# A two-layer decoder on one core: the engines' loop over turns of four tiles written out as one straight program

## The reference, cut to what matters

```python
x = _layernorm(x + _L0_attn_ref(x, ...))             # 16 heads, latent 32, rotary, causal softmax
x = _layernorm(x + _L0_xattn_ref(ctx_1024, x, ...))  # linear attention: q (k^T v), then its own norm
x = _layernorm(x + _L0_ffn_ref(x, ...))              # weights and activations rounded to FP4 blocks, SiLU gate
x = _layernorm(x + _L1_attn_ref(x, ...))             # causal softmax, and a second, moving-average branch
x = _layernorm(x + _L1_xattn_ref(x, ctx_1024, mask, ...))  # masked cross attention, MLP 1024 wide, two norms
x = _layernorm(x + _L1_ffn_ref(x, ...))              # one 256x256 product rounded to FP6 blocks
```

## Time and profile before

| | |
|---|---|
| time, median of 3 runs | 1191.1 us (1190.35 to 1193.04) |
| profiled execution: span | 1188.5 us |
| profiled execution: its own time | not given apart from the span; the median lies 2.6 us above the span |
| ACT, POOL busy | 43%, 26% of the span |
| instructions with a record | 24,029 |
| DMA | mean 21 GB/s |

### The profile page before, as it was taken

The page is one execution under the profiler, slowest core; times in us unless marked ns, Lnnn a source line. Parts: engine busy times, 40 slices in busy tenths (PEclk is TensorE's granted clock), DMA queues, the critical chain, the costliest instruction groups (busy, mean ns, idle before and its releaser), DMA issues.

```text
span 1188.5 us, 24029 instructions
## 1 busy us (share of the span) xinstructions
PE 977.9 (82%) x8390; PEld 759.2 (64%) x8390; DVE 889.0 (75%) x2135; ACT 509.5 (43%) x1377; POOL 309.3 (26%) x507
## 2 busy tenths in 40 slices
PE   6667778898988898988988898988988898978754
PEld 5445656776666676766676776766666666756633
DVE  3775667888788887868788788868787888877452
ACT  2323436363526354453526354453636354443320
POOL 2561111312222232212222232212222232222021
PEclk9677999999999999989999999989999999999886
DMA  9001000000000000000000000000000000000000
GB/s 344 20 10 68 8 13 9 3 20 8 19 8 15 10 17 10 16 9 8 19 7 15 11 16 10 17 13 4 19 7 15 8 6 6 8 6 5 6 5 4
DMA packets 23854, 24.48 MB, mean 21 GB/s; under 512 B 1728, under 2 KB 22064, under 8 KB 23600
## 3 DMA queue, kind: packets, MB, share of 16 engines
q1 hardware_dynamic: 23728, 22.85, 5.9%
HBM read 18.67 MB, written 2.10 MB: 17 GB/s over the span
## 4 chain that ended last, share of the span: by engine, by line
DVE 35%; PE 35%; issue 13%; ACT 10%; POOL 5%; DMA 0%; DVEq 0%; POOLq 0%; SPq 0%
PE bank L1126 26%; PE bank L1239 9%; ACT prob L664 5%; DVE peak L919 4%; DVE y_ L862 2%; DVE ma_ L1038 2%; ACT prob L658 2%; DVE stats L848 2%; DVE q_top L810 2%; DVE k_ L1062 1%; POOL rstd L523 1%; DVE k_ L1071 1%; POOL k_ L531 1%; DVE x_ L874 1%; DVE scratch L822 1%
## 5 line engine op out<-in xcount | busy, mean ns | idle before, releaser
L664 ACT ACTIVATE prob<-bank,low 128x128 f32<-128x128 f32 x384 | 105.2, 385 | 163.9 <-DVE low L926 163.9
L520 POOL TENSOR_TENSOR var_eps<-mean_var,rsq 128x1 f32<-128x1 f32 x144 | 28.5, 198 | 474.8 <-DVE mean_var L851 474.8
L919 DVE TENSOR_REDUCE peak<-bank 128x4 f32<-128x512 f32 x192 | 126.2, 682 | 31.0 <-PE bank L1126 31.0
L1239 PE MATMUL bank<-cst,prob 128*128 128x128 f32 x768 | 108.7, 287 | 49.4 <-DVE y_ L862 30.3
L1239 PEld LDWEIGHTS bank<-cst,prob 128*128 128x128 f32 x768 | 88.0, 146 | 67.2 <-issue 42.9
L602 ACT ACTIVATE xt_<-bank 128x256 f32<-128x256 f32 x144 | 55.2, 396 | 130.9 <-PE bank L1239 130.3
L602 ACT ACTIVATE probT<-bank 128x512 f32<-128x512 f32 x192 | 102.2, 604 | 10.6 <-PE bank L1239 10.6
L523 POOL TENSOR_TENSOR rstd<-var_eps,rsq 128x1 f32<-128x1 f32 x144 | 79.8, 554 | 11.3
L1126 PE MATMUL bank<-w_gu,xt_ 128*128 128x352 f32 x256 | 80.5, 468 | 1.5 <-ACT w_f L602 1.0
L1126 PE MATMUL bank<-xt_,w 128*128 128x128 f32 x512 | 68.6, 299 | 0.5 <-ACT xt_ L602 0.5
L1126 PEld LDWEIGHTS bank<-xt_,w 128*128 128x128 f32 x512 | 68.2, 218 | 0.9 <-ACT xt_ L602 0.9
(11 more groups left out here) (179 smaller groups left out, 2230.1 us busy)
## 6 DMA issues: line engine op xcount, KB each, us to landing
xtin<-in_xT SPq DMA_DIRECT2D x16, 128.0 KB, 2.2
next_<-in_x SPq DMA_DIRECT2D x16, 128.0 KB, 6.7
ct_<-in_ctxT SPq DMA_DIRECT2D x16, 128.0 KB, 7.5
w<-in_w SPq DMA_DIRECT2D x2, 1024.0 KB, 6.2
out<-x_ SPq DMA_DIRECT2D x16, 128.0 KB, 1.7
next_<-x_ SPq DMA_DIRECT2D x16, 127.0 KB
rowt<-in_rows SPq DMA_DIRECT2D x1, 1664.0 KB, 9.1
w<-in_gate_up SPq DMA_DIRECT2D x2, 512.0 KB, 10.4
```

The lines of the kernel that those rows point to most:

```text
L664: ins = act.activation(prob[:, r, c * P:(c + 1) * P], bank[r][:, c * P:(c + 1) * P], ACT.Exp, scale=SCALES[layer], bias=low[:, b, h:h + 1])
L919: dve.tensor_reduce(peak[:, b, 4 * r:4 * r + 4], rows4(src[:, :]), AX_X, ALU.max)\
L1239: ins = pe.transpose(dst[:, k * P:(k + 1) * P], src[:, k * P:(k + 1) * P], ident)
```

## The change

`run` no longer has a loop. It goes once through `TIMELINE`, which holds all sixteen tiles, and calls each stage with the number of the turn and of the tile within it. Since the turn is now always a number, each wait is on a constant and each address is fixed. Stages, their order, buffers, banks and semaphores stay as they are. The parameters of the engine and of the last turn are dropped from the calls.

```diff
-        def run(eng, table, last=ITERS):
-
-
-            for stage, turn, b in steps_in(0):
+        def run(table):
+
+            for _, stage, t in TIMELINE:
                 if stage in table:
-                    table[stage](turn, b)
-            with eng.Fori(1, last) as i:
-                for stage, turn, b in steps_in(1):
-                    if stage in table:
-                        table[stage]((i, turn - 1), b)
-            for stage, turn, b in [step for n in range(last, ITERS + 1) for step in steps_in(n)]:
-                if stage in table:
-                    table[stage](turn, b)
+                    table[stage](t // GROUP, t % GROUP)
...
-            run(sp, table, last=ITERS - 1)
+            run(table)
...
-            run(pool, table)
+            run(table)
...
-            run(act, table)
+            run(table)
...
-            run(dve, table)
+            run(table)
...
-            run(pe, table)
+            run(table)
```

## The result

| | before | after |
|---|---|---|
| time, median of 11 runs each | 1191.1 us (1188.53 to 1197.83) | 1184.83 us (1180.43 to 1187.86) |
| profiled execution: span | 1188.5 us | 1182.7 us (its own time 1184.83) |
| mean granted clock | 0.938 | 0.936 |
| instructions with a record | 24,029 | 22,289 |

The ratio after to before is 0.994, with a 95% interval of 0.9921 to 0.9959. The change makes the kernel faster, by 6.3 us, which is small (0.6%) but clear of the noise. The forecast was 13.5 us (1177.6), and the result lies 1.8 us above its range of 1173.5 to 1183.0. The sign was right, and so was the mechanism of the jumps; more than half of the gain is missing.

What follows compares the result with a forecast made beforehand. It took the kernel as a chain of short hand-overs, no engine full, stalled by loop jumps. Jumps and pattern 13.2 us plus registers 0.3 gave 13.5 us, from 1191.1 to 1177.6 us, range 1173.5 to 1183.0.

Steps and rivals of the forecast that it cites:

- The jumps: Loop end: two jumps back go, 6.4 us each with stalls and slow clock behind, 12.7 us together.
- The registers: Register arithmetic before waits, mostly covered: at most 0.2 us a tile over twelve tiles, 0 to 2.4 us, 0.3 counted.
- What is late next: Slow-clock stretches in turns 2 and 3 after the edit: turn 1's pattern goes on, gain 12.9 to 13.9 us.
- the drain: Code after the last mark, 131.2 us, already straight: change counted as 0, bound two slow stretches, 2.8 us each way.
- D: Turn ends: no change, the stall comes from loading code there and straight code has it too; 1191 us, chance 3%.
- rival E: Turns 1 to 3: longer straight program's code arrives too late, stalls make it slower, about 1335 us; chance 2%.
- The pattern: Tiles of turns 2 and 3: between two of three and three of four long, 518.7 to 519.6 us for eight.
- B: Turns 2 and 3: all tiles come out long at 65.3 us, gain 10.2, time 1180.9 us; chance 14%.
- A: Turn ends: only PE's stall of 6.1 us comes back, the rest is lost in waits; 1185.0 us, chance 7%.
- C: Tiles and drain: more short tiles or a quicker drain, gain 15 to 20, 1171 to 1176 us; chance 12%.

Runs made afterwards that it cites:

- filled kernels: Unread products put in two idle PE gaps (`x1_turn_h`, `l0_mix`) of the straight and loop kernels: 1160.18 us straight, 1173.9 us loop.
- with the pause moved: Straight kernel with 32 or 64 semaphore increments at the start of DVE's program: 1179.96 us and 1180.58 us.
- its repetition: The changed (straight) kernel run again unmodified, beside the kernels with increments: 1183.75 us, ratio 0.9931 to the kernel before.
- one-jump kernel: Against the kernel before, turn 1 also written out, loop covering only turns 2 and 3, one jump back left: 1188.87 us, ratio 0.9985.
- its filled forms: Loop kernel before with unread products in PE's idle gaps: one filling (`x1_turn_h`) 1184.62 us, two fillings (also `l0_mix`) 1173.9 us.
- DVE-only: Against the kernel before, only DVE's program written out straight, other engines keep the loop: 1195.22 us, ratio 1.0004.
- PE-only: Against the kernel before, only PE's program written out straight, other engines keep the loop: 1186.67 us, ratio 0.9926.
- one-iteration loops: Against the kernel before, turns 1, 2 and 3 as three successive loops of one iteration, folded to constants, no branch taken: 1182.85 us, ratio 0.9927.
- The filled kernel: Straight kernel with two fillings, three unread products in `x1_turn_h` and two in `l0_mix`: 1160.18 us, ratio 0.9702 to the kernel before.

## Why the prediction was wrong

**The jumps, 12.7 us: right within 0.8.** Their stalls are gone, and with the slow stretches filled two of them are worth 11.9. What the prediction hadn't seen is how the price is made: PE's stall sets most of it, and DVE's counts in full only once PE's is gone.

**The registers, 0.3 counted of 0 to 2.4: in its bounds, and counted too low for the filled kernels.** A long tile takes 65.13 us without them and 65.39 or 65.32 with them, and in the filled kernels the remainder of 13.9 - 11.9 = 2.0 us over twelve tiles is theirs by subtraction, net of the straight kernel's two pauses. No run changed them alone. That they run beside the operation in progress holds for DVE in the kernel before: 823 of its 852 register instructions lie inside one of its operations.

**The step that failed: "What is late next".** It took turn 1 and its pattern of slow stretches as given for code that is straight, so turn 1 stood in the sum at no change, and it counted the drain as 0. Three terms went against it, 7.7 us together, the whole of the 13.5 - 5.8 that are missing in the spans:

- 2.1 us in one tile of turn 1: the pause of DVE and the slow stretch behind it. This term was not in the sum at all. The passage at 262.9 us was read as proof that new code costs nothing (against D), and rival E priced each of some 17 packets a turn at 3.07 us. What the trace has lies between the two, 0.37 us at a few places, and one such place sufficed.
- 1.9 us in the other tiles, 0.9 of them in turn 1; the other 1.0 is what turns 2 and 3, with a gain of 12.5, lack to the 13.5. One of twelve tiles came out short (63.73), not three or four. This goes with the pause as well: with the pause moved, the twelve tiles take 778.4 and 778.8 us, which is the forecast's 779.0, and with it in place they take 782.95 and 782.67. So the pause is worth 3.9 to 4.5 us over the twelve tiles, about twice what its own tile shows, and it explains all that they lack. How it works on in the later tiles was not traced.
- 3.6 us in the drain, which was counted as 0 with 2.8 as bound. It took three times 3.4 us of slow clock more, not two, in the changed kernel and again in its repetition. Why the drain fell into this pattern stays open.
- The last 0.1 us lies before the first mark.

**The pattern.** Undisturbed it has the time that was forecast, and that is in part luck, since it is not the pattern that was forecast: two tiles of twelve are short, not three or four, and the long ones take 65.1 us, not 65.3. The register time, counted as a gain, works against itself here. A long tile of 65.13 us comes 0.28 us later against the slow stretches, 64.85 apart, where one of 65.35 came 0.5 later, so it takes longer to slip past them. An estimate from these rows: a short tile of 63.73 gives back 1.12, so four long ones go with one short, and twelve tiles take 12 x (4 x 65.13 + 63.73) / 5 = 778.2 us.

**Rivals.** B (all tiles long) is near in its count, eleven of twelve tiles, but not in its time: it gave turns 2 and 3 a gain of 10.2 us, and they have 12.5, since the long tiles are 0.2 us shorter than B took them. A's number, 1185.0, is met by the median within 0.2 us, and its reason is false: no jump's loss stayed behind. C and D are excluded. E is excluded as a sign; that its cause, code that arrives late, is behind the 0.37 us above is inferred from the places of the pauses, and no run shows it.

**A check of size.** Without the pause the edit gives 11.4 and 10.8 us by the medians (1191.4 - 1179.96 and - 1180.58), without most of the slow stretches 13.7. With both in place it gives 6.3, and 7.7 beside the kernels without the pause. No run tells apart what makes up the rest to 13.7.

## What to carry to other kernels

A stall taken out of a kernel in which an engine's clock drops once in each period of the work need not be worth its length: look where the slow stretches fall now, how far each period slips against them, and count as a possible cost any place like PE's wait here, which a pause of 0.37 us lengthened from 0.50 to 0.87 us and behind which a slow stretch then stood in the changed kernel, though none at 0.86 us in the one-jump kernel. To learn what such an edit is worth by itself, compare both versions with the gaps ahead of the slow stretches filled by products that nobody reads. That filling was here worth about four times the edit: 1191.1 us before, 1184.8 straight, 1160.2 straight and filled (in a group in which before took 1193.6).

## What the runs showed of the hardware that was not expected

- A jump back stalled PE by 3.0 to 3.6 us (before, its filled forms, the DVE-only and one-jump kernels) and DVE by 2.6 to 3.1 (before, its filled forms, the PE-only and one-jump kernels), each in its own program. The branch that fell through took 83 ns on PE before; with three such branches the one-iteration loops took 1182.85 us, beside 1184.83 for the changed kernel, so they cost nothing that shows.
- In straight code DVE paused for 0.37 us ahead of its 704th recorded instruction in every kernel in which these are the same, on three chips, and 32 or 64 instructions ahead of it moved the pause (to 449.9 and 660.8 us with 32). The pauses found stand 64 above a multiple of 128 in the count of its records, and most places of that kind show none.
- From 160 us to the last slow stretch, which runs to the end, the stretches at clock 0.50 lasted 3.4, 6.8 or 10.2 us; within a run of periodic tiles they start 64.8 or 64.9 us apart, also when a tile takes 65.1. The filled kernel has none from 157 to 1027 us.
